# A ring of five value blocks, and row maxima negated right behind R

## The reference

```python
q, k, v = heads(x @ Wq), heads(x @ Wk), heads(x @ Wv)   # 16 heads of 64
k, v = concat(mem_k, k), concat(mem_v, v)               # 4 memory tokens ahead of a batch
dots = einsum('bhid,bhjd->bhij', l2norm(q), l2norm(k)) * 10
dots = einsum('hg,bgij->bhij', W_pre_th, dots)          # heads mixed
dots = where(causal, -max, dots); dots = where(dots < 64th largest, -max, dots)
attn = einsum('hg,bgij->bhij', W_post_th, softmax(dots))
out = einsum('bhij,bhjd->bhid', attn, v) * head_scale
return (out * sigmoid(x @ Wg + bg)) @ Wo
```

## Time and profile before

| | us |
|---|---|
| median of 3 runs | 2528.12 |
| runs, least to most | 2526.28 to 2529.97 |
| the profiled execution's own time | 2522.18 |
| its span | 2520.4 |

### The profile page before, as it was taken

The page is one execution under the profiler, slowest core; times in us unless marked ns, Lnnn a source line. Parts: engine busy times, 40 slices in busy tenths (PEclk is TensorE's granted clock), DMA queues, the critical chain, the costliest instruction groups (busy, mean ns, idle before and its releaser), DMA issues. The chain is left out here.

```text
span 2520.4 us, 59240 instructions
## 1 busy us (share of the span) xinstructions
PE 2163.2 (86%) x16115; PEld 1384.9 (55%) x16116; DVE 1912.4 (76%) x7276; ACT 1826.7 (72%) x6082; POOL 1467.1 (58%) x3934
## 2 busy tenths in 40 slices
PE   7995788898898889898989898889888988874997
PEld 3343455665566556555665566556655665554433
DVE  5553489958995899679967996899689968993456
ACT  4442698868886889589968896899689968880543
POOL 2002777577757776777667766777677767750100
PEclk9996799999999999999999999999999999997998
DMA  5001012101210121012101210121012101212001
GB/s 163 0 21 61 19 44 49 41 24 41 56 40 24 40 57 40 24 40 57 40 24 40 57 40 24 40 57 40 24 40 57 40 22 38 55 35 81 1 0 67
DMA packets 112990, 104.93 MB, mean 42 GB/s; under 512 B 34192, under 2 KB 110608, under 8 KB 112656
## 3 DMA queue, kind: packets, MB, share of 16 engines
q1 hardware_dynamic: 107744, 96.64, 15.1%
q10 hardware_dynamic: 4912, 4.46, 0.6%
HBM read 19.13 MB, written 12.71 MB: 13 GB/s over the span
## 5 line engine op out<-in xcount | busy, mean ns | idle before, releaser
L994 PE MATMUL bankC<-R,E 128*128 128x128 f32 x2560 | 358.4, 290 | 53.4 <-POOL R L1364 53.4
L994 PEld LDWEIGHTS bankC<-R,E 128*128 128x128 f32 x2560 | 343.4, 204 | 95.6 <-POOL R L1364 59.8
L978 PE MATMUL bankB<-raw,mixpre 128*128 128x76 f32 (+37 forms) x1024 | 357.2, 437 | 2.7 <-DMA raw<-SC 2.6
L1467 DVE TENSOR_SCALAR S<-S,thr 128x68 f32<-128x68 f32 (+56 forms) x456 | 161.9, 375 | 239.2 <-POOL thr L1357 229.1
L968 PE MATMUL bankD<-KT,QT 64*64 64x258 f32 (+7 forms) x2304 | 197.9, 413 | 128.7 <-ACT SC L1174 95.7
L1219 ACT ACTIVATE E<-S,nmax 128x12 f32<-128x12 f32 (+56 forms) x512 | 239.9, 531 | 93.8 <-POOL nmax L1378 93.7
L1201 ACT ACTIVATE junk<-S,thr 128x68 bf16<-128x68 f32 (+56 forms) x456 | 247.5, 559 | 54.9 <-POOL thr L1346 51.2
L1524 DVE SCALAR_TENSOR_TENSOR E<-S,limit,E 128x68 f32<-128x68 f32 (+56 forms) x456 | 254.3, 593 | 30.4 <-DVE limit L1512 0.5
L1364 POOL TENSOR_SCALAR R<-mixpost,rinv 128x128 f32<-128x128 f32 x512 | 196.8, 391 | 131.3 <-DVE rinv L1528 119.1
L1186 ACT ACTIVATE junk<-bankB 128x68 bf16<-128x68 f32 (+56 forms) x456 | 198.1, 434 | 79.5 <-PE bankB L978 79.4
L1020 PEld LDWEIGHTS bankM<-PT,V 128*64 128x64 f32 x5120 | 182.3, 140 | 102.4 <-issue 84.5
(11 more groups left out here) (173 smaller groups left out, 5059.6 us busy)
## 6 DMA issues: line engine op xcount, KB each, us to landing
X_first<-in_L_attn_x_dram ACTq DMA_DIRECT2D x8, 512.0 KB, 9.7
x<-X_first SPq DMA_DIRECT2D x8, 512.0 KB, 3.0
xt<-x SPq DMA_DIRECT2D x32, 128.0 KB, 2.6
x<-xt SPq DMA_DIRECT2D x32, 128.0 KB, 2.4
X_last<-x SPq DMA_DIRECT2D x8, 512.0 KB, 6.6
out_dram<-X_last SPq DMA_DIRECT2D x8, 512.0 KB, 2.8
raw<-SC SPq DMA_DIRECT2D x8, 258.0 KB, 3.0
raw<-SC SPq DMA_DIRECT2D x8, 254.0 KB, 3.7
```

The costliest lines, as they stand in the source:

```text
L978: last = nc.tensor.matmul(bankB[n % 2][:, 0:wide(n)], W.mixpre[:, :], raw[n % RAWS][:, 0:wide(n)], start=True, stop=True)
L994: last = nc.tensor.matmul(bankC[n % 2][:, jb * P:(jb + 1) * P], E[n % EBUFS][:, jb * P:(jb + 1) * P], R[n % RBUFS][:, :], start=True, stop ...
```

## The change

The five blocks of V become a ring: tile `j`'s values lie in block `j % 5`. The batch's last four tokens are then found in rows 0 to 3 of the next batch's first block, whose halo is now copied for each tile but the first of all. The second half of a batch's last tile multiplies by those rows; afterwards the DMA overwrites them with `mem_v` (at `g == 14` of the new batch's first tile, once the old batch is attended). The rest product stays for the very last tile. The first values of a batch move from `g == 14` to `g == 4` of its first tile, on TensorE ahead of the pair's second `mix`, on ScalarE ahead of the pair's second `evict`. On GpSimd the maxima of `n0 - 2` are negated in iteration `n0` right behind R, where those of `n0 - 4` were negated at its head. `GATES_AT` and `PROJECT_AT` name the places that gates and projection had before; the list `uses` is written as a loop and gives the same order but for the values.

```diff
+V0_AT = 4
+V1_AT = 2
...
         def values_at(t, g):
 
-            if g == 2 and t % TPB == 1:
+            if g == V1_AT and t % TPB == 1:
                 return ("v", t)
-            if g == 14:
-                return {0: ("v", t), 1: ("v", t + 1), 2: ("v", t + 1), 3: ("w", t)}[t % TPB]
+            if g == 14 and t % TPB in ((1, 2) if V1_AT else (0, 1, 2)):
+                return ("v", t + 1)
+            if g == 14 and t == NT - 1:
+                return ("w", t)
             return None
+
+        def early_values(t, g):
+
+            return t % TPB == 0 and g == V0_AT
+
+        def slot(j):
+
+            return j % (TPB + 1)
...
                     if hh:
-                        wait_read(pe, ("w", t, 1) if t % TPB == TPB - 1 else ("v", t + 1, 1))
+                        wait_read(pe, ("w", t, 1) if t == NT - 1 else ("v", t + 1, 1))
...
-                                                    V[:, jb, h * DH:(h + 1) * DH], PT[u % 2][:, jb, h, :],
+                                                    V[:, slot(t - blocks + 1 + jb), h * DH:(h + 1) * DH], PT[u % 2][:, jb, h, :],
...
-                                V[0:MEM, blocks, h * DH:(h + 1) * DH], PTtail[:, h, :],
+                                V[0:MEM, slot(t + 1), h * DH:(h + 1) * DH], PTtail[:, h, :],
...
                     if g == 4:
                         score(2 * t + 1, 2)
+                    if early_values(t, g):
+                        tokens(t, "v", Wv, slice(0, P))
...
             def values(j, what, rows=P):
-                t = j % TPB + (what == "w")
-                if j >= TPB:
-                    act.wait_ge(attended, 2 * (j // TPB * TPB))
+                at = slot(j + (what == "w"))
+                if j > TPB:
+                    act.wait_ge(attended, 2 * ((j - TPB - 1) // TPB * TPB + TPB))
...
+            def memory_values(j):
+                wait_read(act, ("v", j, 1))
+                if j:
+                    act.wait_ge(attended, 2 * j)
+                with nc.allow_non_contiguous_dma("64 columns a head"):
+                    act.dma_start(V[0:MEM, slot(j), :].rearrange("m (h d) -> m h d", d=DH),
+                                  a["mem_v"].rearrange("h m d -> m h d")).then_inc(mem_in, 16)
...
+                    if early_values(t, g):
+                        values(t, "v")
...
+                    if g == 14 and t % TPB == 0:
+                        memory_values(t)
...
-                if j % TPB == 0:
+                if j == 0:
                     nc.gpsimd.memset(dst, 0.0).then_inc(halo, 1)
...
-                if 0 <= n0 - 4 < NG:
-                    m = n0 - 4
-                    pool.wait_ge(max_done, m + 2)
-                    nc.gpsimd.tensor_scalar(nmax[:, ring((m, m + 1))], rmax[:, ring((m, m + 1))], -1.0, 1.0, ALU.mult,
-                                            ALU.mult).then_inc(nmax_ready, 2)
                 if ranked_in(n0 - 2):
                     second_threshold(ranked_in(n0 - 2))
...
                 for n in (n0 - 6, n0 - 5):
                     if 0 <= n < NG:
                         scaled_mix(n)
+                if 0 <= n0 - 2 < NG:
+                    m = n0 - 2
+                    pool.wait_ge(max_done, m + 2)
+                    nc.gpsimd.tensor_scalar(nmax[:, ring((m, m + 1))], rmax[:, ring((m, m + 1))], -1.0, 1.0, ALU.mult,
+                                            ALU.mult).then_inc(nmax_ready, 2)
```

More of the change, by code:

```diff
@@ L28 @@
 GBUFS = 3
+PROJECT_AT = 8
+GATES_AT = (6, 6, 6, 6)
+V0_AT = 4
+V1_AT = 2
 LAG = 8
@@ L816, in attention_phase @@
             ahead = t + 1 < NT
[L817 to L828, removed]
+            for g in range(0, GPT, 2):
+                if g == 0 and ahead:
+                    uses += [("xT", t + 1, 0)] + two("q", t + 1)
+                if g == 2:
+                    uses += score_steps(2 * t + 1, 0) + score_steps(2 * t + 1, 1)
+                if g == 4:
+                    uses += score_steps(2 * t + 1, 2)
+                if early_values(t, g):
+                    uses += two("v", t)
+                if g == 4 and ahead:
+                    uses += two("k", t + 1)
+                if g == 6:
+                    uses += score_steps(2 * t + 1, 3)
+                if g == 8 and ahead:
+                    uses += two("qT", t + 1) + two("kT", t + 1)
+                if g == 10 and ahead:
+                    uses += score_steps(2 * t + 2, 0)
+                if g == 12 and ahead:
+                    uses += score_steps(2 * t + 2, 1) + score_steps(2 * t + 2, 2)
+                if g == 14 and ahead:
+                    uses += score_steps(2 * t + 2, 3)
+                if g == gates_turn(t):
+                    uses += two("g", t)
+                if values_at(t, g):
+                    uses += two(*values_at(t, g))
         place = {u: i for i, u in enumerate(uses)}
@@ L1087, in _ @@
                         score(2 * t + 2, 2)
-                    if g == 6:
+                    if g == gates_turn(t):
                         gates(t)
@@ L1095, in _ @@
                             tokens(j, "w", Wv, slice(P, P + MEM), MEM)
-                if g == 8 and 2 <= t < NT:
+                if g == PROJECT_AT and 2 <= t < NT:
                     project(t - 2)
@@ L1129, in values @@
             def values(j, what, rows=P):
-                t = j % TPB + (what == "w")
-                if j >= TPB:
-                    act.wait_ge(attended, 2 * (j // TPB * TPB))
+                at = slot(j + (what == "w"))
+                if j > TPB:
+                    act.wait_ge(attended, 2 * ((j - TPB - 1) // TPB * TPB + TPB))
                 for half in range(2):
                     act_use(act, (what, j, half), lambda: nc.scalar.copy(
[L1135 to L1138, removed]
-                        act.dma_start(V[0:MEM, 0, :].rearrange("m (h d) -> m h d", d=DH),
-                                      a["mem_v"].rearrange("h m d -> m h d")).then_inc(mem_in, 16)
+                        V[0:rows, at, half * 512:half * 512 + 512], bankD[0:rows, half, :]))
+            def memory_values(j):
[5 more added lines that the diff above has]
+                                  a["mem_v"].rearrange("h m d -> m h d")).then_inc(mem_in, 16)
             def gates(j):
```

3 lines of the change are left out of this document (added).

## The result

The changed kernel takes 2514.15 us in the median of 20 runs; the kernel before, on the same chip, 2530.69 us in 20. The ratio is 0.9931, with a 95% interval of 0.9915 to 0.9946: 0.7% faster, some 17 us. The profiled execution took 2512.08 us around a span of 2510.2.

The account below looks back on a forecast made before the run. The bound moves: VectorE in a batch's last tile, a path between GpSimd, TensorE and ScalarE in earlier tiles. Terms - 12.0 - 4.5 + 3.0 + 1.6 = - 11.9 us gave 2516.2 us; range 2503 to 2531 us.

Parts of the forecast that it names:

- the eighth pair: First tile of each batch: removing the first values' product there saves 9.45 us in batches 1 to 7, 12.0 together.
- the early maxima: Row maxima negated right behind R: 4.5 us saved at seven batch changes, 3.0 us lost at norms of k.
- What bounds the kernel, and the rest products: Last tile of a batch: VectorE sets the time, so removing seven rest products, 25.2 us of TensorE's work, gains 0.
- The rival of TensorE as the bound: Everywhere: TensorE sets the time, so the rest products count in full, 25.2 us more: 2491 us; chance 0.07.
- the signs of being wrong: Third pair's k scores later than before, last tile shorter, or ScalarE's early time returning as a longer wait for thresholds.
- 1.35 us for each of batches 1 to 7: First tile's eighth pair: without the values' product ScalarE's count starts 1.35 us earlier and what follows keeps that: 9.45 us.
- The values in the third pair: First tile of a batch: the value product goes where TensorE waits 3.02 us for R; k product ends at 1530.4.
- the slower rival: Third pair: the value product comes onto the path in full, 8 x 3.67 = 29.4 us: 2548 us; chance 0.13.
- 0.83 us is gained, not 1.5 and not 5.7: Change of batch: ScalarE's wait ends 5.7 us earlier, but GpSimd's mask of group 7 had waited only 0.83 us.
- 0.19 for the norm: Change of batch: negated maxima now stand ahead of the norm of k on GpSimd, costing 0.19 us, net gain 0.64.
- The first batch: Third pair there: no gap for the value product, so scores behind k start 1.4 us later, + 1.6 with the norm.
- The rule against the edit: Maxima's new place beside VectorE's shifts: the shared-port lock could stretch them, losing 7.9 us: 2524 us; chance 0.08.

Follow-up runs that it names:

- the two sets: The changed kernel timed twice against the kernel before on the same chip: 2514.15 us, ratio 0.9931, and again 2521.69 us, ratio 0.9954.
- the second profile: Profile of the changed kernel, unaltered, from its second timing against the kernel before: 2521.69 us, ratio 0.9954.
- the second product: Changed kernel with the first values' product done again in the eighth pair, besides the third: 2520.02 us, 0.995 against the kernel before.
- The delay: Changed kernel with five small GpSimd instructions ahead of group 6's mask in the first tile of batches 1 to 7: 2533.87 us, 1.0003 against the kernel before.
- set 4: Runs sharing a chip: two fill, projection and delay variants of the changed kernel against the kernel before, which took 2532.16 us.
- the rest-kept program: Changed kernel with the rest product put back into the eighth pair of every fourth tile: 2563.46 us, 1.0122 against the kernel before.

## Why the prediction was right

The time came in the range, and near the forecast: the medians of the two sets fell by 16.5 and 10.3 us where the sum has - 11.9. But the sum came near because two terms were off in opposite ways, and that is luck: the eighth pair gave much less than its 12.0 us, and the early maxima much more than their 1.5.

**What bounds the kernel, and the rest products: right.** 0 us for 25.2 of TensorE's work, borne out by the kernel before without six of the seven. The last tile keeps its 52.6 of 55 us of VectorE:

```profile
1463.00:1518.00 55.00, 49.01 (x489) 35.35 (x488) 52.61 (x174) 43.18 (x123) 29.47 (x81) 0.94 0.04 10
```

The rival of TensorE as the bound (2491 us) falls with it. The last tile did not stay quite as it was: from last reciprocal to last reciprocal it takes 78.9 us in the mean of batches 1 to 6 (78.8 in the second profile), where it took 77.6, and VectorE waits 2.6 us for thresholds in it instead of 1.4. The first three tiles together became 3.3 us shorter (1.2 in the second profile). And one of the signs of being wrong did appear, a longer wait for thresholds: ScalarE waits 88 us less for maxima, but 28 us more for first thresholds.

**The eighth pair: mis-sized.** The step "1.35 us for each of batches 1 to 7" read the count rightly (0.30 us behind its threshold), and the q product starts 1.34 us sooner after the turn. In the first batch, count and threshold stand at 288.90 and 288.60, where the earlier trace rows have 290.66 and 287.83: the 2.54 us are there. What failed is that "what follows", the q product among it, would keep its duration. TensorE arrived early at scores that SyncE had only begun to gather at 1292.10, waited 2.06 us, and did the q product at a lower clock, 1.2 us longer, so that it ends 0.13 us sooner. Instead of 12.0 us, the second product puts this term at 5 us or nothing, and its profile puts it in the first batch alone. The row to add was the gather's landing, which the removed product had covered. That the lower clock comes of that wait is only in part shown: in the second profile the mix behind the same wait of 2.06 us takes 0.51 us, not 0.84, and the q product is slow all the same (4.64).

**The values in the third pair: right with the other edit, wrong alone.** With early maxima the scores behind k wait for nothing. I had the k product end at 1530.4 - 1523.9 = 6.5 us after R; it ended 5.4 after: the values' product began 0.5 us sooner ahead of R, and the mix lay beside other work. Without early maxima the slower rival's place was real: the ring and the values alone gained nothing. How much of that the third pair cost by itself no run tells, since that run has the eighth pair's gain in it too.

**The maxima: right in place, mis-sized by the clock.** The step "0.83 us is gained, not 1.5 and not 5.7" less 0.19 for the norm gave 0.64 us; the rows after have 0.74. GpSimd's stretch from R to turned k in the second tile became 0.19 us longer, as forecast: 5.64 us from this R to 1344.12 before,

```profile
1338.48 0.73 POOL L1364 TENSOR_SCALAR R<-mixpost,rinv 128x128 f32<-128x128 f32 x2
```

and 5.83 from this one to the turn at 1330.23 after.

```profile
1324.40 0.72 POOL L1404 TENSOR_SCALAR R<-mixpost,rinv 128x128 f32<-128x128 f32 x2
1325.09 0.19 POOL L1428 TENSOR_SCALAR nmax<-rmax 128x2 f32<-128x2 f32 x1
...
1328.23 1.95 POOL L1359 TENSOR_TENSOR qk<-qk,rn 128x1024 f32<-128x1024 f32 x1
```

So by its own steps the edit is worth 1.5 us. Alone it gave 11.4. The term counted "a batch change, 7 x" and left the first batch to the values' term; 4.4 us lie there, by the profiles. Some 7 us are left for the other batches. Part of them lies with products that meet the full clock again: the values of the second tile (5.2 to 5.4 us before, 3.67 with the maxima moved, in five of eight batches; in batch 7 it went the other way) and the k product in the third pair (4.77 in batch 2 before, 3.60 then; two later batches went the other way). The delay shows the same from the other side, 0.78 us for 1.8 or 2.6. That the clock is the amplifier is read from these durations and from the table; no run held the clock fixed. The kernel before varies with the clock by itself: in set 4 its three runs at a clock of 0.939 took 2543.5 to 2544.4 us, and its three at 0.949 or more took 2524.4 to 2528.9.

A second reason is untested. VectorE's masking of a row takes 0.65 us at this width, but 2.29 beside GpSimd's norm product. In the kernel before:

```profile
707.88 0.65 DVE L1524 SCALAR_TENSOR_TENSOR E<-S,limit,E 128x412 f32<-128x412 f32 x1
708.45 2.29 DVE L1524 SCALAR_TENSOR_TENSOR E<-S,limit,E 128x420 f32<-128x420 f32 x1
```

```profile
708.18 2.11 POOL L1319 TENSOR_TENSOR qk<-qk,rn 128x1024 f32<-128x1024 f32 x1
710.26 0.53 POOL L1378 TENSOR_SCALAR nmax<-rmax 128x2 f32<-128x2 f32 x1
```

Twenty maskings take over 1.5 us in the kernel before, 15 with the maxima moved and 14 in the changed kernel, all beside that product; the maskings of the third tile hardly meet it any more (6 times before, once after, in batches 1 to 6). VectorE's maskings take 7.7 us less in all with the maxima moved, 9.6 less in the changed kernel. How much of it is on the path no run shows: the ring and the values alone had 14 such maskings and gained nothing.

**The first batch: its start right, its sum too small.** The scores behind k came at 259.62 instead of 258.52, + 1.1 where I had + 1.4. But the batch as a whole ends 4.2 us earlier (3.5 in the second profile), where the two terms for it sum to 1.6 - 2.54 = - 0.9 us: across the eighth pair the reciprocals gain 4.7 us (4.6), not 2.54. Part of that is again the clock: the values' product behind it, in the second tile, takes 3.67 us where it took 5.2.

```profile
251.03 3.67 PE L959 MATMUL bankD<-Wv,xnT 128*128 128x512 f32 x8 [0.58 <-ACT SC L1210]
254.70 3.66 PE L959 MATMUL bankD<-Wk,xnT 128*128 128x512 f32 x8
...
259.62 0.46 PE L999 MATMUL bankD<-KT,QT 64*64 64x132 f32 x8 [1.09 <-ACT qk L1160]
```

**The rule against the edit.** In the new place the negated maxima take 183 to 303 ns, 192 in the median, where the earlier trace rows have 185, 526 and 193. The lock of the Trainium skill ("SBUF — State Buffer", "Who interferes with whom") would stretch them beside VectorE's shifts, but I had the place wrong: none of them runs beside a shift, before or after, and the nearest is over 0.7 us away. What had stretched them was in the old place. 26 of 256 took over 210 ns in the kernel before, 20 of these beside the masking with its two inputs in SBUF, as the one of 0.53 us shown above; 5 did in the changed kernel. So the trace agrees with the rule's two inputs, the edit took the maxima away from them, and that rival falls.

**Open** are the 5 us between the two measurements of the changed kernel, the size of the terms in question, how the maxima's gain divides between the clock and VectorE's maskings, and why the rest-kept program fetches instructions for so long.

## What to carry to other kernels

Before you take out work that seems to hold an engine up, ask what else arrives at that moment: the product removed had covered a gather, and in the later batches its gain turned into a wait for it and a slower product behind. Price a step on the path by what it covers and by what it fills; moving a 3.6 us projection into a wait of 2 us, in 29 tiles, was worth 33 to 41 us, at least twice the whole change. And where small terms decide, measure each part alone, and each kernel in more than one profile: here the sum was right and its two main terms were wrong, and two profiles of one kernel put the end of attention 17.6 us apart.

## What the runs showed of the hardware

- TensorE's granted clock changes the duration of a product by more than the shift that a small edit makes. A delay of 0.78 us a batch cost 1.8 or 2.6. The same product behind the same three waits (0.29, 0.26 and 1.89 us) took 3.67 us at 1055.36 in the changed kernel and 5.37 at 1066.75 in the one before.
- Filling TensorE's wait with products of its own raised the clock of the next product and lowered that of the one after. The Trainium skill ("TensorE: Matmul & The Clock Gate", "HAM oscillation — how this bites in real kernels") tells of waits between TensorE's pieces of work that make each next piece start slow. The trace agrees for the mix and the q product behind the wait of 2.06 us in the first profile (0.84 and 4.88 us; 0.40 and 3.67 before); that filling such a wait only moved the fall is this case's.
- VectorE's masking, which has two inputs in SBUF, took 2.29 us instead of 0.65 beside GpSimd's norm product, and a GpSimd instruction of 0.19 us took 0.53 beside that masking.
- One program stood some 42 us behind attention while its instructions came in, without an edit there. A kernel's time can hold such a piece, and only a look at the stretches tells it from the edit's effect.
